# Attention output projection in two halves, each behind the transposes of its own 128 tokens

## The reference

```python
x = x + layernorm(attn(layernorm(x), wq, wk, wv, wo))
x = x + layernorm(ffn(layernorm(x), theta, phi, theta_noise, phi_noise))

# attn: 16 heads of 64, window 256: a block of 256 queries sees its own
# and the previous block of keys, banded; softmax in float32
q, k, v = x @ wq.T, x @ wk.T, x @ wv.T
out = softmax(mask(q k^T / 8)) v ;  return out @ wo.T

# ffn
real = x @ cos(theta + theta_noise);  imag = x @ sin(phi + phi_noise)
return sqrt(real**2 + imag**2)
```

## Time and profile before

| what | us |
|---|---|
| median of 2 runs | 4000.62 |
| the two runs | 3992.12 and 4009.12 |
| the profiled execution, whole | 3997.06 |
| its span on the slowest core (core 0) | 3995.5 |
| spans of the 8 cores | 3971.8 to 3995.5 |
| PE busy, share of the span | 80% |
| DVE busy | 42% |
| ACT busy | 34% |

### The profile page before, as it was taken

One profiled execution on the slowest core, in us unless ns is written; L12 is line 12 of the kernel. 1 busy time (PEld: TensorE's weight loads), 2 busy tenths in 40 slices (PEclk: granted clock), 3 DMA queues, 4 the chain that ended last, 5 costly groups with the idle time before them and its releaser, 6 DMA issues.

```text
span 3995.5 us, 52090 instructions; the slowest of 8 cores (3971.8 to 3995.5 us)
## 1 busy us (share of the span) xinstructions
PE 3213.8 (80%) x19808; PEld 2117.0 (53%) x19808; DVE 1664.9 (42%) x3632; ACT 1371.1 (34%) x2176; POOL 112.2 (3%) x215
## 2 busy tenths in 40 slices
PE   0009888989888898988889798988889898888985
PEld 0006555566555555655555555655555665555562
DVE  2222436172543617254361617254361725436162
ACT  3333333242433324242342424243332424334241
POOL 1100000000000000000000000000000000000000
PEclk6558998989899898989989798989989898988987
DMA  6774241514223151423315141422415142331503
GB/s 214 233 256 164 92 161 64 180 52 169 106 105 148 64 190 42 169 106 116 141 61 205 70 171 62 169 106 94 160 64 181 52 169 106 116 143 59 208 14 137
DMA packets 54164, 511.27 MB, mean 128 GB/s; under 512 B 5792, under 2 KB 5920, under 8 KB 28576
## 3 DMA queue, kind: packets, MB, share of 16 engines
q0 software_dynamic: 30384, 266.35, 17.9%
q1 hardware_dynamic: 23536, 241.58, 17.0%
HBM read 465.97 MB, written 41.94 MB: 127 GB/s over the span
## 4 chain that ended last, share of the span: by engine, by line
PE 68%; DVE 19%; issue 5%; DMA 5%; ACT 2%; DVEq 0%; POOL 0%; SPq 0%; ACTq 0%; POOLq 0%
PE pb L519 34%; PE pb L464 18%; PE pb L672 5%; DVE attn_sb L703 5%; DVE stats L700 5%; PE pb L772 5%; DVE ao_sb L814 2%; PE pb L662 2%; PE pb L734 2%; DMA wsc<-pl 2%; PE pb L404 1%; DVE attnT_sb L745 1%; DVE sc L852 1%; DVE pl L228 1%; DVE sc L938 1%
## 5 line engine op out<-in xcount | busy, mean ns | idle before, releaser
L700 DVE TENSOR_REDUCE stats<-pb 128x1 f32<-128x384 f32 (+2 forms) x512 | 269.6, 527 | 819.6 <-PE pb L672 819.6
L772 PE MATMUL pb<-v_sb,attnT_sb 128*128 128x64 f32 x2880 | 488.0, 314 | 97.0 <-DVE attnT_sb L745 95.3
L772 PEld LDWEIGHTS pb<-v_sb,attnT_sb 128*128 128x128 f32 x2880 | 446.2, 230 | 170.6 <-issue 167.9
L714 ACT ACT_TABLE_LOAD x256 | 328.4, 1283 | 534.8 <-DVE attn_sb L703 534.5
L464 PE MATMUL pb<-fmh,slot0h 128*128 128x256 bf16 x1024 | 279.8, 273 | 270.2 <-DMA slot0l<-wsc 270.2
L519 PE MATMUL pb<-slot2h,fmh 128*128 128x512 bf16 x992 | 375.9, 379 | 13.4 <-ACT ao_sb L909 13.4
L519 PE MATMUL pb<-slot2h,fml 128*128 128x512 bf16 x992 | 375.9, 379 | 0.0
L519 PE MATMUL pb<-slot2l,fmh 128*128 128x512 bf16 x992 | 375.9, 379 | 0.0
L464 PE MATMUL pb<-fmh,slot1h 128*128 128x256 bf16 x960 | 276.4, 288 | 88.8 <-DVE sc L852 88.8
L703 DVE TENSOR_SCALAR attn_sb<-pb,stats 128x384 f32<-128x384 f32 (+2 forms) x512 | 303.7, 593 | 56.0 <-DVE stats L700 1.4
L417 ACT ACT_TABLE_LOAD x32 | 41.1, 1283 | 826.8 <-PE pb L404 826.8
(11 more groups left out here) (114 smaller groups left out, 4740.6 us busy)
## 6 DMA issues: line engine op xcount, KB each, us to landing
slot0h<-wsc SPq DMA_DIRECT2D x33, 2048.0 KB, 10.3
slot1h<-wsc SPq DMA_DIRECT2D x33, 2048.0 KB, 11.1
slot0l<-wsc POOLq DMA_DIRECT2D x33, 2048.0 KB, 13.1
slot1l<-wsc POOLq DMA_DIRECT2D x33, 2048.0 KB, 14.2
slot2h<-wsc SPq DMA_DIRECT2D x33, 2048.0 KB, 10.7
slot2l<-wsc POOLq DMA_DIRECT2D x33, 2048.0 KB, 13.6
x_sb<-x POOLq DMA_DIRECT2D x32, 512.0 KB, 6.2
y<-sc POOLq DMA_DIRECT2D x32, 512.0 KB, 3.8
```

Of the source, the lines that this page charges most:

```text
L700: ev[f"mx_{g}_{uu}"] = ve.inc(vector.reduce_max(stats[:, P + up:P + up + 1], kept, axis=AX.X))
L714: ev[f"ex_{g}_{uu}"] = ac.inc(scalar.activation(attn_sb[:, up * SL:up * SL + (c1 - c0 + 1) * 128], attn_sb[:, up * SL:up * SL + (c1 - c0 + ...
L772: ins = tensor.matmul(pb[b_av][:, (h % 8) * DH:(h % 8 + 1) * DH], lhsT, rhs, start=(first_in_bank and ci == 0), stop=(last_in_bank and ci ...
```

## The change

The normalisation is done in two groups of one reciprocal (16 columns) and 16 multiplies, one group for each token tile, and both bundles of a token tile's transposes wait for its whole group. The output projection is emitted in two parts, `op0` (tiles 0 and 1) and `op1` (tiles 2 and 3): `op0` stands between `aot0` and `aot1` in the code, so that on TensorE the second token tile's transposes come behind tiles 0 and 1. The next block's first layer norm stays behind `aot1`. The order on VectorE and ScalarE is not changed but for the merged groups.

```diff
         def emit_tsplit_tt(g, ht, src_sb, tag, waits=(), banks=(0, 1),
-                           dsth=None, dstl=None, bi_waits=None):
+                           dsth=None, dstl=None):
...
         def emit_proj_tm(g, use_id, tag, hi_ev, lo_ev, banks, extra_waits=(),
-                         srch=None, srcl=None, tile_waits=None, kc_tag=None):
+                         srch=None, srcl=None, tile_waits=None, kc_tag=None,
+                         tile0=0):
...
-                tt, nh = ti // 2, ti % 2
+                tt, nh = (tile0 + ti) // 2, (tile0 + ti) % 2
...
-            ev[f"use_mm_{use_id}"] = ev[f"{tag}_mm3"]
+            ev[f"use_mm_{use_id}"] = ev[f"{tag}_mm{len(banks) - 1}"]
...
             for qsub in range(2):
                 avb = [0, 1] if qsub == 0 else [2, 3]
-                for hh in range(2):
...
-                        kb.wait(vector, ac, ev[f"ex_{g}_{u_last}"])
-                        kb.wait(vector, mm, ev[f"av_{g}_{u_last}"])
-                        ev[f"rc_{g}_{qsub}_{hh}"] = ve.inc(vector.reciprocal(
-                            stats[:, c0:c0 + 8],
-                            stats[:, P + 8 + qsub * 16 + hh * 8:
-                                  P + 16 + qsub * 16 + hh * 8]))
-                        kb.wait(vector, ve, ev[f"rc_{g}_{qsub}_{hh}"])
...
+                    kb.wait(vector, ac, ev[f"ex_{g}_{u_last}"])
+                    kb.wait(vector, mm, ev[f"av_{g}_{u_last}"])
+                    ev[f"rc_{g}_{qsub}"] = ve.inc(vector.reciprocal(
+                        stats[:, P + 40 + qsub * 16:P + 56 + qsub * 16],
+                        stats[:, P + 8 + qsub * 16:P + 24 + qsub * 16]))
+                    kb.wait(vector, ve, ev[f"rc_{g}_{qsub}"])
+                    ins = None
+                    for h in range(H):
...
-            emit_tsplit_tt(g, 0, ao_sb, f"aot0_{g}", banks=(0, 1),
-                           bi_waits=[[(ve, ev[f"ao_{g}_0_0"])],
-                                     [(ve, ev[f"ao_{g}_0_1"])]],
+            emit_tsplit_tt(g, 0, ao_sb, f"aot0_{g}",
+                           waits=[(ve, ev[f"ao_{g}_0"])], banks=(0, 1),
                            dsth=fmh2, dstl=fml2)
...
+            o_use = 3 + 6 * g
+            _ow0 = [(ac, ev[f"aot0_{g}_hi"]), (ve, ev[f"aot0_{g}_lo"])]
+            emit_proj_tm(g, o_use, f"op0_{g}", None, None, [0, 1],
+                         tile_waits=[_ow0, _ow0],
+                         srch=fmh2, srcl=fml2)
+
+            h_ev2, l_ev2 = emit_tsplit_tt(g, 1, ao_sb, f"aot1_{g}",
+                                          waits=[(ve, ev[f"ao_{g}_1"])], banks=(2, 3),
                                           dsth=fmh2, dstl=fml2)
 
             if not last:
                 emit_ln1(g + 1, g_waits=[(mm, ev[f"aot1_{g}_tp1"])])
 
-            o_use = 3 + 6 * g
-            _ow0 = [(ac, ev[f"aot0_{g}_hi"]), (ve, ev[f"aot0_{g}_lo"])]
             _ow1 = [(ac, ev[f"aot1_{g}_hi"]), (ve, ev[f"aot1_{g}_lo"])]
-            emit_proj_tm(g, o_use, f"op_{g}", h_ev2, l_ev2, [0, 1, 2, 3],
-                         tile_waits=[_ow0, _ow0, _ow1, _ow1],
+            emit_proj_tm(g, o_use, f"op1_{g}", None, None, [2, 3],
+                         tile_waits=[_ow1, _ow1], tile0=2,
                          srch=fmh2, srcl=fml2)
             pump_loads(o_use + 4)
```

More of the change, by code:

```diff
@@ L345, in _ @@
                     kb.wait(tensor, qc, ev["cst"])
-                    if bi_waits is not None:
-                        for c_, v_ in bi_waits[bi]:
-                            kb.wait(tensor, c_, v_)
                     for c_, v_ in waits:
@@ L821, in build_nc @@
-                ev[f"ao_{g}_{qsub}"] = ev[f"ao_{g}_{qsub}_1"]
-            emit_tsplit_tt(g, 0, ao_sb, f"aot0_{g}", banks=(0, 1),
-                           bi_waits=[[(ve, ev[f"ao_{g}_0_0"])],
-                                     [(ve, ev[f"ao_{g}_0_1"])]],
-                           dsth=fmh2, dstl=fml2)
-            h_ev2, l_ev2 = emit_tsplit_tt(g, 1, ao_sb, f"aot1_{g}", banks=(2, 3),
-                                          bi_waits=[[(ve, ev[f"ao_{g}_1_0"])],
-                                                    [(ve, ev[f"ao_{g}_1_1"])]],
+                u_last = qsub * 16 + 15
@@ new lines, in _ @@
+                @block.vector
+                def _(vector, qsub=qsub, u_last=u_last):
+                    kb.wait(vector, ac, ev[f"ex_{g}_{u_last}"])
[6 more added lines that the diff above has]
+                    for h in range(H):
+                        b_av = avb[h // 8]
+                        rcol = P + 40 + qsub * 16 + h
+                        ins = vector.tensor_scalar_mul(
+                            ao_sb[:, qsub * 1024 + h * DH:qsub * 1024 + (h + 1) * DH],
+                            pb[b_av][:, (h % 8) * DH:(h % 8 + 1) * DH],
+                            stats[:, rcol:rcol + 1])
+                    ev[f"ao_{g}_{qsub}"] = ve.inc(ins)
@@ new lines, in build_nc @@
+                kb.bank_set(avb, [(ve, ev[f"ao_{g}_{qsub}"])])
+            emit_tsplit_tt(g, 0, ao_sb, f"aot0_{g}",
+                           waits=[(ve, ev[f"ao_{g}_0"])], banks=(0, 1),
+                           dsth=fmh2, dstl=fml2)
+            o_use = 3 + 6 * g
[3 more added lines that the diff above has]
+                         srch=fmh2, srcl=fml2)
@@ L850, in _ @@
                 for ti in range(4):
-                    kb.wait(vector, mm, ev[f"op_{g}_mm{ti}"])
+                    otag = f"op0_{g}" if ti < 2 else f"op1_{g}"
+                    kb.wait(vector, mm, ev[f"{otag}_mm{ti % 2}"])
                     ins = vector.tensor_copy(
@@ L893, in build_nc @@
                                        banks=(4, 5, 6, 7),
-                                       hi_waits=[(mm, ev[f"op_{g}_mm3"])],
+                                       hi_waits=[(mm, ev[f"op1_{g}_mm1"])],
                                        dsth=fmh2, dstl=fml2)
```

## The result

The changed kernel takes 4064.19 us (median of all executions) against 4001.4 us for the kernel before, measured side by side. Now and then an execution of either kernel is disturbed on one die (four cores); such executions are left out of all ratios, single times are given where too few are left for an interval, and of the profiled execution of `f7_fill_both`, in which cores 4 to 7 were disturbed, only cores 0 to 3 are read. On the executions that are left (before 3990.83 to 4009.12 us, mean 3995.4; after 4062.06 to 4066.35, mean 4063.9) the ratio is 1.0172, with a 95% interval of 1.0156 to 1.0187. The profiled execution took 4063.82 us (span 4062.3), which is 66.8 us over the profiled one of before (3997.06), or 4.2 us for each of the 16 blocks. The prediction's sum was 3.52 us a block.

A forecast was written before the change was run, and what follows sets the result against it. TensorE's matmuls were taken to set the time. A 4.11 us stall less a 0.59 us earlier start, 3.52 us in 16 blocks, adds 56 us: 4053 to 4057, said as 4055 us (1.4% more), range 4030 to 4092.

The forecast's parts named there:

- The prediction's sum: Per block: 4.11 us stall before tile 2 less 0.59 us earlier projection start, 3.52 us; chance 0.62 as it stands.
- The stall of 4.11 us before tile 2: TensorE waits through second-half transposes, table load, copies and low halves; 4.11 us a block, 3.0 of them idle.
- The earlier start: Two fewer VectorE reciprocals let low halves end and the projection start 0.59 us sooner per block.
- The table load: ScalarE's load before the second half's copies stays, 1.28 of the 4.11 us stall.
- the 4033 us that the rule gives: Rival: ScalarE's second table load goes away, leaving 2.24 us a block, 36 us in all; chance 0.03.
- What moves along: Next block's first layer norm, 7.4 us, moves beside tiles 2 and 3, ending some 2.8 us early; cost zero.
- paid for downstream: Rival: the K projection's 5.9 us wait shortens, leaving only the 0.59 us gain, 3988 us; chance 0.07.
- The clock in the hole: No TensorE clock fall before tile 2, zero cost; rival, falling in most blocks, about 4092 us, chance 0.18.
- The clock at the head of the projection: Cold start costing 2.5 us a block stays; rival, a warm start, 4013 us, chance 0.06.
- nothing is won there: zero: Moving second-half transposes from ahead of the projection gains at most 0.04 us, as VectorE's low halves end unchanged.
- the expectation for e1: Set before that run: about 4007 us if the tile 2 wait is the loss, about 4060 if coarser groups are.

The follow-up runs named there:

- f7_fill_both: Changed kernel plus 8 transposes nobody reads ahead of the projection and 24 more in the hole before tile 2; ratio 1.0077.
- f3: Changed kernel with the second half's transposes one tile sooner, between projection tiles 0 and 1; 4004.5 us, ratio 1.0024.
- e2: Kernel before with only the new order of projection and transposes, keeping its four normalisation groups; 4058.32 and 4061.86 us.
- e4: Changed kernel plus eight transposes nobody reads between `aot0` and `op0`; 4053.79 us, ratio 1.0149.
- f5: Kernel before, nothing merged, plus three transposes nobody reads behind each of the first three transpose bundles; 3963.03 us, ratio 0.9919.
- e1: Changed kernel with only the merged normalisation kept, transposes and projection back in the old order; 3958.44 us, ratio 0.9915.
- g9: f3 plus eight transposes nobody reads ahead of `op0`; 3958.84 us, ratio 0.9896.
- g8: e1 plus 40 transposes nobody reads in TensorE's idle time before the K projection; 3955.06 us, ratio 0.9886.
- g10: g9 plus 40 transposes nobody reads in TensorE's idle time before the K projection; 3972.43 us, ratio 0.9933.

## Why the prediction was right

The time lies in the range, and the way and the size are near the sum: 4055 forecast, 4064.19 measured; 56 us more forecast, 68.5 measured by the means above. Point by point:

- *The stall of 4.11 us before tile 2.* Right: 668.04 to 672.15 is 4.11 in the block shown, idle 3.07 (forecast 3.0), and 4.12 is the mean over the blocks. It was put together from rows of other transposes, because it is the same string of work. f3 shows that it carries the loss: with cover for it, 1.0172 becomes 1.0024.
- *The earlier start.* Forecast 0.59 us, measured 8.4 / 16 = 0.52. Right but for some hundredths, and e2, which starts no sooner than before, bears out that the moved transposes win nothing there by themselves.
- *The table load.* Kept, and there: `L369 ACT_TABLE_LOAD`, 1.28 us, in the middle of the stall (668.72). By the rule of the Trainium skill, "ScalarE: Activation LUTs", section "Table sets: the hidden batching unit", a copy behind a copy needs none; the trace differs again, as in the earlier trace rows, and the 4033 us that the rule gives are not met.
- *What moves along.* The layer norm of the next block runs beside tiles 2 and 3, from 671.92 to 679.36, and nothing waits for it: the transposes that need it start at 682.67. The wait before the K projection stays at 5.9 us, so nothing is paid for downstream; the transposes behind tile 3 moved with it, as argued.
- *The clock in the hole.* Forecast no fall, from 2.73 us of idle at the head of the attention; it fell in 22 of 128 blocks, 0.59 us of low clock a block on the mean, so 0.3 us of time. Right in the main, but partly by luck: the forecast went by the length of the idle time, and that alone does not decide. In e4 the same hole brings the clock down in 96 of 128 blocks; in the changed kernel it stayed up in 105 of the 111 blocks whose `op0` had spent 4 us or more at the low clock, and of what `op0` does to it the prediction said nothing.
- *The clock at the head of the projection*: the term that was mis-sized. The prediction took the cold start as it was and gave it some 10 us either way in the range. Its low clock went from 3.95 to 4.88 us a block, since the second half's transposes no longer stand right ahead of it and TensorE idles there for 2.68 us (with that idle time filled, in e4, it is 1.42): 16 x 0.93 / 2 = 7.4 us. With the 16 x 0.59 / 2 = 4.7 us of the falls in `op1` that is 12.2 us; with the 1.0 us that the earlier start gave less, it is the 13 us by which the sum (56 us) is short of the measured stages (77.9 - 8.4 = 69.5; the last instructions of the slowest cores lie 66.8 apart).

The step that would have warned of it stands in the prediction as "nothing is won there: zero": the second half's transposes ahead of the projection were costed at nothing because VectorE's low halves end as late. They cost nothing, but they were worth something, as f5 shows: work on TensorE right ahead of the projection shortens its cold start. The same step made the expectation for e1 miss, where the projection gains 14 us with the same sixteen transposes drawn together ahead of it; that they are the reason there is likely, but no run shows it by itself.

## What to carry to other kernels

Before splitting a matmul stage so that its first part can start sooner, look at what the second part's operands pass through: here transposes, a table load, copies and low halves, 4.11 us in a row, which had been free beside the first part's wait and were not any more. If such a split is wanted, leave enough matmuls that need nothing new between the second part's transposes and the second part itself, as f3 does with one tile. And price the work that a change takes from in front of a stage not only by what it occupies but by the clock at which the stage then starts.

## What the runs showed of the hardware

- Transposes on TensorE ahead of a matmul stage shorten its time at the low clock: 3.95 to 1.02 us a block with nine unread ones in the gaps (f5), 5.05 to 1.05 with eight (g9); 40 of them keep the granted clock at 1.00 through the idle time before the K projection (g8), where it had fallen to 0.50. The Trainium skill, "TensorE: Matmul & The Clock Gate", section "Part 4: PE-mode transpose", says that the high clock does not engage for transposes, which are not counted as busy in the same way. These float32 transposes differ from that: in e4 the clock was 0.50 at the first of them and 1.00 at the projection's first matmul in 82 of 128 blocks. The traces list them as matmuls with the identity and do not tell whether that mode was on.
- Whether the clock falls in a hole depends on more than the hole. The same 3.07 us of idle after the same eight transposes were followed by a fall in 73 of the 82 blocks whose `op0` had run at the high clock from its first matmul, and in none of the 21 whose `op0` had spent 4 us or more at the low one (e4).
- Low clock saved in the K projection came back in the attention: 24.1 us less in the K projection, 22.5 us more in the attention (g8 against e1), and 22.7 against 20.9 in g10 against g9. Why the attention pays stays open. Its time also differs between profiled executions whose attention is the same code: 1275.8 us before, 1262.0 in e2. So the 15.1 us that e1's attention is shorter can't be put down to the merged groups with the same certainty as the projection's 13.6.
